# A two-layer retention kernel: the last slot's sums between other products, its last mask in PSUM and bf16, and the first inputs in another order

## The reference

```python
scores = einsum('bsd,d->bs', hidden, w_router)
top_scores, top_idx = top_k(scores, 256)        # of the 512 tokens of a batch
weights = sigmoid(top_scores)
out = hidden
out[top_idx] += weights * (gelu(hidden[top_idx] @ W1 + b1) @ W2 + b2)
```

## Time and profile before

| what | value |
|---|---|
| median of 3 runs | 825.61 us (825.09 to 827.93) |
| profiled execution, time | 823.52 us |
| profiled execution, span of the trace | 821.7 us |
| TensorE busy | 760.8 us |
| VectorE busy | 671.2 us |
| GpSimd busy | 475.2 us |
| ScalarE busy | 425.0 us |

### The profile page before, as it was taken

The page is one execution under the profiler, slowest core; times in us unless marked ns, Lnnn a source line. Parts: engine busy times, 40 slices in busy tenths (PEclk is TensorE's granted clock), DMA queues, the critical chain, the costliest instruction groups (busy, mean ns, idle before and its releaser), DMA issues.

```text
span 821.7 us, 29578 instructions
## 1 busy us (share of the span) xinstructions
PE 760.8 (93%) x13003; PEld 617.1 (75%) x13003; DVE 671.2 (82%) x1825; ACT 425.0 (52%) x875; POOL 475.2 (58%) x374
## 2 busy tenths in 40 slices
PE   4777999999999999998789999999999999999685
PEld 3656888888788788776578888878788888887553
DVE  3678888888888999986747889987777898988777
ACT  1334556565555455664444446655544456545634
POOL 3278888888887888776323444534434434444514
PEclk9798999999999999999999999999999999999998
DMA  7000110000101100010000000000000000000113
GB/s 228 28 28 29 28 28 28 6 25 28 28 29 29 28 28 2 3 54 2 1 2 2 3 2 3 2 2 2 2 3 2 2 2 2 2 3 28 41 38 103
DMA packets 23426, 18.63 MB, mean 23 GB/s; under 512 B 2161, under 2 KB 20610, under 8 KB 23042
## 3 DMA queue, kind: packets, MB, share of 16 engines
q1 hardware_dynamic: 22594, 16.21, 6.7%
q10 hardware_dynamic: 704, 0.54, 0.2%
HBM read 12.55 MB, written 4.19 MB: 20 GB/s over the span
## 4 chain that ended last, share of the span: by engine, by line
PE 74%; DVE 16%; POOL 4%; ACT 3%; issue 1%; DMA 1%; DVEq 0%; SPq 0%; ACTq 0%; POOLq 0%
PE ps L281 20%; PE ps L405 11%; PE ps L396 10%; PE ps L276 5%; PE ps L659 4%; POOL grstd L1051 3%; PE ps L292 3%; PE ps L359 3%; PE ps L379 3%; PE ps L303 2%; PE ps L389 2%; DVE x L1207 2%; PE ps L351 2%; PE ps L651 2%; PE ps L315 2%; PE ps L669 1%
## 5 line engine op out<-in xcount | busy, mean ns | idle before, releaser
L1051 POOL TENSOR_TENSOR grstd<-gve,mhalf 128x32 f32<-128x32 f32 (+1 forms) x32 | 159.0, 4968 | 27.7 <-DVE gve L1262 27.7
L405 PEld LDWEIGHTS ps<-w_s,hid 128*128 128x128 f32 x1024 | 126.5, 196 | 8.3 <-issue 7.2
L405 PE MATMUL ps<-w_s,hid 128*128 128x128 f32 x1024 | 131.5, 281 | 0.0
L396 PE MATMUL ps<-xt_r,w_s 128*128 128x512 f32 x256 | 126.6, 617 | 0.7 <-ACT xt_r L805 0.7
L809 ACT ACTIVATE hid<-ps,b_s 128x512 f32<-128x512 f32 x128 | 84.1, 726 | 25.7 <-PE ps L396 25.7
L1047 POOL TENSOR_TENSOR r_ret<-ve_ret,powers 128x8 f32<-128x8 f32 x32 | 57.8, 1807 | 32.0 <-DVE ve_ret L1193 32.0
L1042 POOL TENSOR_TENSOR rstd_ln_mod<-ve_ln_mod,mhalf 128x4 f32<-128x4 f32 x32 | 32.3, 1010 | 73.5 <-DVE ve_ln_mod L1193 73.5
L1057 POOL TENSOR_TENSOR um<-um 128x96 f32<-128x96 f32 (+1 forms) x32 | 21.3, 666 | 90.3 <-DVE um L1241 90.3
L281 PE MATMUL ps<-w_qkvg,xt_p 128*128 128x128 f32 x512 | 70.4, 282 | 2.8 <-ACT xt_p L805 2.8
L396 PEld LDWEIGHTS ps<-xt_r,w_s 128*128 128x128 f32 x256 | 45.1, 191 | 35.3 <-issue 30.7
L1235 DVE TENSOR_TENSOR sc<-ps,tri 128x1024 f32<-128x1024 f32 (+1 forms) x64 | 58.3, 953 | 16.0 <-PE ps L315 9.5
(11 more groups left out here) (232 smaller groups left out, 1755.8 us busy)
## 6 DMA issues: line engine op xcount, KB each, us to landing
out_x<-base SPq DMA_DIRECT2D x16, 256.0 KB, 2.3
xin<-in_x SPq DMA_DIRECT2D x15, 256.0 KB, 3.1
xtin<-in_xt SPq DMA_DIRECT2D x15, 256.0 KB, 3.8
rot<-in_rot SPq DMA_DIRECT2D x2, 1024.0 KB, 7.3
w_s<-in_w SPq DMA_DIRECT2D x2, 256.0 KB
xin<-in_x ACTq DMA_DIRECT2D x1, 256.0 KB, 6.8
w_qkvg<-in_wqkvg SPq DMA_DIRECT2D x1, 256.0 KB, 7.0
xtin<-in_xt ACTq DMA_DIRECT2D x1, 256.0 KB, 9.9
```

The lines of the kernel that those rows point to most:

```text
L396: nc.tensor.matmul(bank(k), w1_s[:, f, :], xt["r"][:].rearrange("p j n -> p (j n)"), start=True, stop=True).then_inc(s[f"h{f}"], 1)
L405: mm = nc.tensor.matmul(bank(k, j * P, P), hid[:, f, j * P:(j + 1) * P], w2_s[:, f, :], start=False, stop=(f == last and j == NT - 1), ski ...
L1051: nc.gpsimd.tensor_tensor(grstd[:, 0:n], gve[:, 0:n], mhalf[:, 0:n], ALU.pow) \
```

## The change

Opening: SP issues `xtin[0]` second and the bias as a single row of 128 values; PE spreads that row over the partitions in a product with a row of 0.5, between the product L415 and the product L418. DVE copies the result later, and its layernorm statistics move behind the halving of `w_ffn`. The centring of `w_qkvg` moves behind the first `tilewise`.

Last slot: the sums of the fourth search move to other places between PE's products, two of them ahead of DVE's `scaled_sum`; POOL waits for `gy` ahead of the additions 3 to 5 and takes addition 5 ahead of a root; `keep_base` and `rank_mask` move forward. The last scan's mask lies in PSUM bank 3 (with a new wait for ACT's last `hidden`), the scan starts from the count, so that one step on the count is gone, and the last mask and its right-hand side are bfloat16. Two tensor_tensor operations on 128x1 operands become tensor_scalar operations.

```diff
                 load(lead[:].rearrange("p a n -> p (a n)"), lead_d, "w_lead_in")
-                load(bias_b[:], all_rows(bias), "w_bias_in")
+                sp.dma_start(xtin[0][:], xt_d[0]).then_inc(s["xt_in0"], 16)
+                load(bias_r[:], bias.rearrange("(a n) -> a n", a=1), "w_bias_in")
                 load(w_qkvg[:].rearrange("p a n -> p (a n)"), wqkvg0, "w_qkvg_in")
...
+            pe.wait_ge(s["w_bias_in"], 16)
+            pe.wait_ge(s["w_half"], 1)
+            nc.tensor.matmul(bank(2, 0, P), half_r[:], bias_r[:], start=True, stop=True).then_inc(s["w_pe"], 1)
             pe.wait_ge(s["w_step"], W_KERNEL)
             nc.tensor.matmul(bank(3, 0, P), cen, w_ffn[:], start=True, stop=True).then_inc(s["w_pe"], 1)
-            pe.wait_ge(s["w_qkvg_in"], 16)
...
+            def centre_first():
+                pe.wait_ge(s["w_qkvg_in"], 16)
...
-            def last_mask(src, k, first):
+            def last_mask(src, to, k, first):
...
+                if g < 0:
+                    centre_first()
                 if sl.prepare:
                     wait(pe, "x1", new)
...
                 transpose_gated(now, YB)
+                rank_sum(3, 3, 1)
                 wait(pe, "act0", old)
                 routed_up(2, X1)
-                output_b(now)
-                rank_sum(3, 3, 1)
+                output_b(now, (0, 1))
+                rank_sum(3, 4, 1)
+                output_b(now, (2, 3))
                 wait(pe, "act1", old)
                 routed_up(3, 3)
+                rank_sum(3, 5, 1)
                 last_rows(LAST, YB)
                 routed_down(0, 2, old)
-                rank_sum(3, 4, 1)
                 routed_down(1, 2, old)
                 wait(pe, "x2", now)
                 last_column(LAST, 0)
-                rank_sum(3, 5, 1)
...
                 last_rows(NB - 1, YB)
+                rank_mask(3, YB + 1)
                 last_column(NB - 1, 0)
                 wait(pe, "act2", old)
                 routed_up(0, X1)
-                rank_mask(3, YB + 1)
...
-                last_mask(msk_a, 0, True)
+                last_mask(msk_a, rs[:, TAB - 2:TAB], 0, True)
                 wait(pe, "k_mask", 5)
-                last_mask(srow, 0, False).then_inc(s["k_mt"], 1)
+                last_mask(picked, sel_b[:], 0, False).then_inc(s["k_mt"], 1)
...
-            act.dma_start(xtin[0][:], xt_d[0]).then_inc(s["xt_in0"], 16)
...
+            nc.gpsimd.memset(half_r[:], 0.5).then_inc(s["w_half"], 1)
...
                 group_root(4 * H1, now)
-                add_output(3)
-                add_output(4)
+                wait(pool, "gy", now)
+                for n in range(3, 6):
+                    add_output(n)
                 root("ln_mod", now)
-                for n in range(5, len(BY_ACT)):
+                for n in range(6, len(BY_ACT)):
...
-                rank_step(nc.vector.tensor_tensor(thr, rs[:, r:r + 1], lo, ALU.add))
+                rank_step(nc.vector.tensor_scalar(thr, rs[:, r:r + 1], lo, None, ALU.add))
...
-                rank_step(nc.vector.tensor_tensor(nxt, low, ahead, ALU.add))
+                rank_step(nc.vector.tensor_scalar(nxt, ahead, low, None, ALU.add))
...
-            def last_choice(k, r, kr):
+            def last_choice(k, r, kr, kb):
+                wait(dve, "act3", 2 * NB)
...
-                rank_step(nc.vector.scalar_tensor_tensor(msk_b[:], bank(k), lo, msk_a[:], ALU.is_ge, ALU.subtract))
-                rank_step(nc.vector.tensor_scalar(cnt, cnt, -1.0, float(TOPK), ALU.mult, ALU.add))
-                rank_order()
-                rank_step(nc.vector.scalar_tensor_tensor(srow[:], srow[:], cnt, msk_b[:], ALU.is_le, ALU.mult), "k_mask")
+                rank_step(nc.vector.scalar_tensor_tensor(bank(kb), bank(k), lo, msk_a[:], ALU.is_ge, ALU.subtract))
+                rank_order(bank(kb), cnt)
+                rank_step(nc.vector.scalar_tensor_tensor(picked[:], srow[:], float(TOPK), bank(kb), ALU.is_le, ALU.mult), "k_mask")
...
-            dve.wait_ge(s["w_bias_in"], 16)
-            step(nc.vector.tensor_scalar(bias_b[:], bias_b[:], 0.5, None, ALU.mult))
...
-            input_statistics(0, 16, 1)
             dve.wait_ge(s["w_pe"], 3)
+            step(nc.vector.tensor_copy(bias_b[:], bank(2, 0, P)))
+            assert steps[0] == W_BIAS
+            dve.wait_ge(s["w_pe"], 4)
             step(nc.vector.tensor_scalar(w_ffn[:], bank(3, 0, P), 0.5, None, ALU.mult))
             assert steps[0] == W_FFN
+            input_statistics(0, 16, 1)
...
+                step(nc.vector.tensor_copy(sel_b[:], rs[:, TAB - 2:TAB]))
...
                 rank_try(4)
+                rank_narrow(3, 4, 1)
+                rank_try(5)
                 wait(dve, "base", old)
                 scaled_sum(BT["wo"], r_ret[sl.buf(0, 4)][:, 0, :], x1[sl.buf(0, 4)], x2, "wo", "x2", now)
                 variance("ln_mod", x2, ve["ln_mod"], now)
-                rank_narrow(3, 4, 1)
-                rank_try(5)
-                negative_mean(now)
                 rank_narrow(3, 5, 1)
                 rank_above()
+                negative_mean(now)
                 rank_between()
                 rank_order()
                 rank_choose()
+                keep_base(sl.batch(0), now)
                 last_load(YB)
...
                 last_next(1)
-                keep_base(sl.batch(0), now)
```

More of the change, by code:

```diff
@@ L108, in program @@
         wr_c = sb("wr_c", [P, 1])
+        picked = sb("picked", [P, S], BF16)
+        sel_b = sb("sel_b", [P, 2], BF16)
         wr_f = sb("wr_f", [P, FEW])
@@ L115, in program @@
         bias_b = sb("bias_b", [P, P])
+        bias_r = sb("bias_r", [1, P])
+        half_r = sb("half_r", [1, P])
         amax = sb("amax", [P, 5])
@@ L416, in _ @@
                 .then_inc(s["w_pe"], 1)
+            pe.wait_ge(s["w_bias_in"], 16)
+            pe.wait_ge(s["w_half"], 1)
+            nc.tensor.matmul(bank(2, 0, P), half_r[:], bias_r[:], start=True, stop=True).then_inc(s["w_pe"], 1)
             pe.wait_ge(s["w_step"], W_KERNEL)
             nc.tensor.matmul(bank(3, 0, P), cen, w_ffn[:], start=True, stop=True).then_inc(s["w_pe"], 1)
-            pe.wait_ge(s["w_qkvg_in"], 16)
-            pe.wait_ge(s["w_step"], W_VALUE)
-            nc.tensor.matmul(bank(2), cen, w_qkvg[:].rearrange("p a n -> p (a n)"), start=True, stop=True) \
-                .then_inc(s["w_pe"], 1)
+            def centre_first():
+                pe.wait_ge(s["w_qkvg_in"], 16)
+                pe.wait_ge(s["w_step"], W_VALUE)
+                nc.tensor.matmul(bank(2), cen, w_qkvg[:].rearrange("p a n -> p (a n)"), start=True, stop=True) \
+                    .then_inc(s["w_pe"], 1)
             def centre_rest():
@@ L835, in keep_rest @@
             def keep_rest():
-                act.wait_ge(s["w_pe"], 5)
+                act.wait_ge(s["w_pe"], 6)
                 nc.scalar.copy(w_qkv1[:], bank(3)).then_inc(s["w_act"], 1)
@@ L1348, in rank_between, with rank_order @@
                 rank_step(nc.vector.tensor_scalar(cnt, cnt, -1.0, float(TOPK), ALU.mult, ALU.add))
-            def rank_order():
-                rank_step(nc.vector.tensor_tensor_scan(srow[:], msk_b[:], zero[:].to_broadcast((P, S)), 0.0, ALU.add,
+            def rank_order(src=msk_b[:], first=0.0):
+                rank_step(nc.vector.tensor_tensor_scan(srow[:], src, zero[:].to_broadcast((P, S)), first, ALU.add,
                                                        ALU.add))
@@ L1427, in _ @@
             step(nc.vector.tensor_copy(peaks, amax[:, 0:1].to_broadcast((P, P))))
-            dve.wait_ge(s["w_bias_in"], 16)
-            step(nc.vector.tensor_scalar(bias_b[:], bias_b[:], 0.5, None, ALU.mult))
-            assert steps[0] == W_BIAS
             dve.wait_ge(s["w_pe"], 1)
@@ L1690, in slot_end @@
                 last_narrow(3, X2)
-                last_choice(YB, 3, X2)
+                last_choice(YB, 3, X2, 3)
                 last_weigh(0)
@@ L1698, in _ @@
             run_slots(slot_a, slot_ab, slot_b, slot_end)
-W_BIAS = 3
-W_KERNEL = W_BIAS + 7
-W_FFN = W_KERNEL + 1
+W_KERNEL = 2 + 7
+W_BIAS = W_KERNEL + 1
+W_FFN = W_BIAS + 1
 W_VALUE = W_FFN + 3
-W_SCALE = W_VALUE + 5
+W_SCALE = W_VALUE + 6
 W_STEPS = W_SCALE + 8
```

6 lines of the change are left out of this document (3 added, 3 removed).

## The result

| what | before | after |
|---|---|---|
| median of 4 runs each, same chip | 826.58 us (825.09 to 827.93) | 815.27 us (813.06 to 815.59) |
| ratio of the times | | 0.9866 [0.9839, 0.9894] |
| profiled execution, time | 823.52 us | 813.06 us |
| profiled execution, span | 821.7 us | 811.1 us |

The account below looks back on a forecast made before the run. PE (93% busy) bounds the middle, DVE's chain most of the last slot, the bias wait the opening. 3.6 + 0.3 + 1.75 + 2.45 + 1.25 + 0.45 - 0.9 = 8.9 us; 825.6 - 8.9 = 816.7, range 814.3 to 820.0.

Parts of the forecast that it names:

- Opening, 3.6 forecast: Opening: without the repeated bias row's wait, the copy to `xt_p` starts at 13.5 instead of 17.14, 3.6 us saved.
- I take 6.6: Opening: the single bias row lands at 6.6, between bounds of 4 and 11.6, and its product ends at 7.15.
- Middle, 0.3 forecast: Middle: L1331 as tensor_scalar loses its stretching, most of it under PE's cover; 0.3 us saved, bounds 0 and 2.3.
- Last slot to the first narrow, 1.75 forecast: Last slot: the first narrow moves from 802.61 to 800.85 by moved sums and an undisturbed `nmr`; 1.75 us saved.
- behind them (784.8): Last slot: the sum DVE got at 788.08 stands behind the gated transposes, at 784.8, and DVE narrows at 785.1.
- no wait over 1 us of DVE for a sum: Sign for the last slot: DVE never waits over 1 us for a sum, where it once waited 3.60.
- Narrow rounds, 2.45 forecast: Last slot: three rounds at the undisturbed 1.68 take 5.05 instead of 7.51; 2.45 us saved, 0.7 of it `keep_base`.
- Rival (c): Tensor_scalar forms still meet POOL; 1.85 of the narrow rounds and the middle's 0.3 come back: 818.9, chance 0.05.
- Choice, 1.25 forecast: Last slot: count step gone (0.19) and scan 1.23 instead of 2.33; 1.25 us saved, bounds 1.2 and 2.4.
- Last mask, 0.45 forecast: Last slot: the last mask's products, half as many in bf16, take 0.45 for 1.07; 0.45 us saved.
- Tail, 0.9 lost: Kernel's end: `output(NB - 1)` meets POOL's last addition and stores crowd; 0.9 us lost, bounds 0 and 2.3.
- Rival (b): Tail: POOL's and SP's last outputs end the kernel, only 3 us of the last slot come through: 818.7, chance 0.12.

Follow-up runs that it names:

- e11_centring_back: The kernel after with the centring of `w_qkvg` ahead of the first `tilewise` on PE again: 821.09 us, ratio 0.9939.
- e4_pool_first: The kernel after with POOL's `weighted_output` of batch 13 ahead of addition 6 and SP's store order matched: 813.22 us, ratio 0.9845.
- e6_pool_order_back: The kernel after without POOL's wait for `gy` and with addition 5 behind the root again: 815.81 us, ratio 0.9893.
- e7_sums_back: The kernel after with PE's sums 3 to 5 and DVE's narrow, trial and `nmr` in the order of before: 815.93 us, ratio 0.9901.
- e8_mask_in_sbuf: The kernel after with the last scan's mask in SBUF again and no wait for `hidden`: 816.95 us, ratio 0.9903.
- e1_opening: The kernel before with only the change's opening, last slot as before: 820.03 us, ratio 0.992.
- e3_tensor_tensor: The kernel after with both small tensor_scalar operations as tensor_tensor again: 814.62 us, ratio 0.986.
- e2_last: The kernel before with only the change's last slot part, both tensor_scalar forms included: 820.83 us, ratio 0.9931.
- e9_xtin_on_act: The kernel after with `xtin[0]` issued third on ACT's queue, as before, the single bias row staying: 816.62 us, ratio 0.9886.

## Why the prediction was right, and where its sizes were off

**Opening, 3.6 forecast, 4.9 measured.** The chain was the right one: no bias wait, `tilewise` ahead of the centring, the statistics off the path to `w_ffn`. The step that was mis-sized is the landing of the bias row, "I take 6.6", nearest to the repeated row. It was there by 4.79, and the product behind it, taken at 0.45, was two passes of 0.79 together; neither was waited for. L426 ran at 6.27 instead of 7.15. That and the centring, 1.70 instead of 2.05, make 1.2 of the 1.3 by which `xt_p` beat the 13.5. Part of this is the luck of one execution: the seven other profiles of this opening run L426 at 6.47 to 6.59 and have `xt_p` at 12.55 to 13.13, between 4.0 and 4.6 under 17.14. The repeated row was a bad yardstick, since it was one large transfer of 64 KB and the new row is 512 bytes. The wait for it was named first, but `e11_centring_back` shows that its removal alone would not have brought the 3.6: with the centring ahead of `tilewise` and everything else new, `xt_p` is only 0.66 under before.

**Middle, 0.3 forecast, 1.4 measured.** The step failed in its cause. Six of the 18 trials lost a stretch of some 0.35 us and the other twelve took 50 ns more. The start of `x1` in the two kernels is 5.8 us apart ahead of the trials and 5.6 behind the first six, so the new form lost 0.2 there; it stays at 6.3 across the other twelve. The 1.4 come from PE's half rate, which no edit touches. Between the start of `xt_p` and the rank load after took 743.7 us and before 745.1; `e4_pool_first`, `e6_pool_order_back`, `e7_sums_back` and `e8_mask_in_sbuf`, with the code of after up to there, took 743.6 to 745.7. So the 1.4 lies within what one code shows from profile to profile: it is luck, and the 1.1 above the forecast has no cause in the change. The same stretch of PE's program lies in these windows (columns: us, busy and count of PE, PEld, DVE, ACT, POOL, then the granted clock), before:

```profile
24.00:36.00 12.00, 10.12 (x181) 8.52 (x181) 7.46 (x28) 3.29 (x6) 3.63 (x6) 0.58 0.15 47
```

and after, where PE gets through 274 matrix products against 181 in 12 us:

```profile
19.00:31.00 12.00, 9.82 (x274) 8.31 (x262) 7.89 (x30) 3.28 (x6) 3.88 (x6) 0.86 0.15 47
```

A granted clock of 0.58 is mostly 1.2 GHz, one of 0.86 mostly 2.4. The lower rate starts at nearly the same point of PE's program, from 25.8 before and from 21.4 after; ahead of it PE was busy for 5.55 us with the same pauses in both (of 8.0 from 17.8, and of 8.5 from 12.9). But it lasts 10.2 us before and 3.4 after, and no run shows why. This brought 1.5 us by 37 us; 0.8 of it was lost again up to the change of layers, the 0.2 of the trials included, and 0.7 came at that change.

**Last slot to the first narrow, 1.75 forecast, 1.2 measured.** The order of the steps held: `nmr` 0.16, two sums ahead of `wo`, no DVE wait of 3.6. The mis-sized term is PE's product ahead of the fourth sum: "behind them (784.8)" counted the gated transposes at 1.04, but PE was at half rate there (granted clock 0.50 from 772.3 to 779.1) and L663 took 1.79, so that DVE waited 2.29. `scaled_sum` starts 27.3 us after the rank load's first reduction, as before (27.2), and not 0.9 sooner. The gain comes behind it: the sixth trial is done by then, so that the narrowing and `rank_above` fill the wait for POOL's root, and `nmr` takes 0.16. The forecast said "no wait over 1 us of DVE for a sum", and that was wrong by its own times: with L1657 at 1.2 the trial ahead ends near 783.5, and the sum was put at 785.1. `e7_sums_back` puts the whole move at 2.15 us and `e6_pool_order_back` the POOL part at 0.9; together 3.0, more than the 1.2 seen against before. Two things stand against it: `keep_base`, moved here at 0.7, and PE's rate; that the two explain the whole difference is argued, not shown. For the latter `e1_opening` is the measure, with the code of before and half-rate transposes (1.91): from the rank load to the first narrow it took 41.5 us where before took 40.4, after 39.2 and `e7_sums_back` 41.6.

**Narrow rounds, 2.45 forecast, 2.3 measured.** The size was right and the cause partly wrong. The prediction had all three rounds at "the undisturbed one", with the tensor_scalar as the reason that nothing stretches. `e3_tensor_tensor` shows that the place does it, not the form. Rival (c), "the tensor_scalar forms still meet POOL", did not happen: in the narrow rounds POOL was not there, and where it was, at 776.05 in the kernel after, the tensor_scalar took 0.21 and the tensor_tensor of `e3_tensor_tensor` 1.25. The sign "L1331 never over 0.2" was missed by the form's own price, 0.21. In the trials of the middle the tensor_tensor is stretched up to 553 ns and the tensor_scalar never. By the Trainium skill, VectorE: DVE Perf Modes, section "What auto-detection actually checks", one-source operations within SBUF could take a 2-port mode; at one element these 24 rows show no sign of a lock.

**Choice, 1.25 forecast.** Count step (0.19), scan (1.05) and the mask's product (0.06) make 1.3. `e8_mask_in_sbuf`, which keeps the count step out, gives 1.3 back, because there the product is stretched as well (1.57), which it was not before (0.75). The new wait for ACT's `hidden` was met. **Last mask, 0.45 forecast, 0.8 measured:** the four bf16 products took 0.25 together, less than the 0.45 taken for them, and PE was ready for them.

**Tail, 0.9 lost, 1.3 measured.** The mechanism was the one named: DVE's `output` and POOL's last addition meet. They cost 0.8 (final addition 11.1 earlier where `last_weigh` is 11.9 earlier), and the stores at the end another 0.5. `e4_pool_first` gives 1.1 of the stretch back, with the tail at 5.0 us as before. Rival (b), by which only 3 us of the last slot come through, falls: `e2_last` alone shows 4.4 by its stretch (55.1 for 59.5) and 5.7 by its ratio.

## What to carry to other kernels

Where a chain passes through several inputs, each late for a moment, list what is late next after every edit; the gain comes when the last of them is moved, and no single edit has a share of it that could be added up. Before a difference of 1 us is put down to an edit, look at the same stretch in other profiles of the same code: here one opening varied by 0.9 us and one middle by 2.1. When two engines share a port, first move their work apart or put one operand in PSUM, and price another form of the instruction at its own duration: here it was free of a stretch of 1.04 us, which a wait for PE covered anyway, and cost 0.05 each time, 0.2 over the narrow rounds. An engine that is early at one place and in the way at another, as POOL's last pair was, is to be given that work in its idle time.

## What was not expected of the hardware

**A scalar read from a tile costs.** A tensor_scalar of 128x1 with its scalar from a tile takes 206 to 214 ns, a tensor_tensor of the same size 152 to 160 where it is not stretched, and a tensor_scalar with a constant 156 to 158.

**A repeated row slows its neighbours.** 64 KB read as one row of 512 bytes for each of 128 partitions took 5.1 us; the single row, with 256 KB ahead of it, was there 3.1 us after its issue at 1.65. `xin` and `w_qkvg`, in flight at the same time, took 6.8 and 7.0 us beside the repeated row, 4.0 and 3.8 after, and 3.8 and 3.4 in `e9_xtin_on_act`, which issues the first transfers in the order of before and differs there only in the row's form.

**Equal products at unequal rates.** The first 32 products on `xt_p` take 3.81 us after and 5.54 in `e8_mask_in_sbuf`, whose edit lies 790 us later. The timelines of the two, after and then `e8_mask_in_sbuf`:

```profile
12.96 3.81 PE L286 MATMUL ps<-w_qkvg,xt_p 128*128 128x128 f32 x32 [0.77 <-ACT xt_p L818]
```

```profile
13.78 5.54 PE L286 MATMUL ps<-w_qkvg,xt_p 128*128 128x128 f32 x32 [0.77 <-ACT xt_p L818]
```

The same holds in `e2_last`, `e3_tensor_tensor`, `e9_xtin_on_act` and `e11_centring_back` (6.17, 5.73, 5.71 and 6.37), though the records give a granted clock of 1.00 for these stretches in all five. The first use of these products is 1.7 us later in `e8_mask_in_sbuf` than in `e6_pool_order_back`, which has `xt_p` at the same time. What decides it stays open. It may be part of why runs of one kernel spread by 1 to 5 us, and it is why the stretches were compared and not the medians alone.
